# The first tile's rows chosen from the ranks, and the tile tables worked out beside that tile

## What is computed

```python
for d in range(depth):                      # depth 4, so 16 leaves
    logits = xf @ Wr[off:off + cnt].T + br[off:off + cnt]
    sel = take_along_axis(logits, leaf)
    leaf = leaf * 2 + (sel > 0)
h = gelu(xf @ W1[leaf] + b1[leaf])          # 512 -> 2048
y = h @ W2[leaf] + b2[leaf]                 # 2048 -> 512
out = x + y                                 # each row by its own leaf's expert
```

## Time and profile before

| | us |
|---|---|
| median of 3 runs | 629.48 |
| lowest and highest | 628.8 and 632.06 |
| profiled execution, its time | 632.86 |
| its span, first to last instruction | 630.9 |
| PE busy in the span | 549.9 |
| DVE busy | 191.2 |
| ACT busy | 162.4 |
| POOL busy | 62.1 |

### The profile page before, as it was taken

One profiled execution on the slowest core, in us unless ns is written; L12 is line 12 of the kernel. 1 busy time (PEld: TensorE's weight loads), 2 busy tenths in 40 slices (PEclk: granted clock), 3 DMA queues, 4 the chain that ended last, 5 costly groups with the idle time before them and its releaser, 6 DMA issues.

```text
span 630.9 us, 9966 instructions
## 1 busy us (share of the span) xinstructions
PE 549.9 (87%) x3098; PEld 288.6 (46%) x3098; DVE 191.2 (30%) x597; ACT 162.4 (26%) x548; POOL 62.1 (10%) x88
## 2 busy tenths in 40 slices
PE   2877787889899999998599999978898788987994
PEld 1544555543447466444355555524444244443352
DVE  5997776661520100266611111100111001110100
ACT  1667777111201011003022222211222012210311
POOL 3000000030000000000021121111101111011021
PEclk9979999999999999999799999988999799897998
DMA  5169900000201010023069999999999999999940
GB/s 116 13 229 431 404 3 16 18 0 1 84 3 65 0 66 0 10 60 104 1 245 422 420 425 419 426 424 426 428 426 418 422 429 425 420 422 424 428 157 5
DMA packets 24917, 145.66 MB, mean 231 GB/s; under 512 B 10303, under 2 KB 12553, under 8 KB 16706
## 3 DMA queue, kind: packets, MB, share of 16 engines
q1 hardware_dynamic: 21698, 142.91, 55.1%
q0 software_dynamic: 3200, 2.50, 2.0%
HBM read 142.38 MB, written 4.72 MB: 233 GB/s over the span
## 4 chain that ended last, share of the span: by engine, by line
PE 53%; DMA 24%; DVE 8%; ACT 6%; issue 5%; ACTq 2%; POOL 0%; SPq 0%; DVEq 0%; POOLq 0%
DMA w<-in_L_ffn_W 24%; PE P L913 15%; PE P L809 8%; PE P L961 7%; PE P L819 7%; PE P L828 3%; ACT H L513 2%; ACT H L507 2%; PE P L663 2%; PE P L930 2%; DVE stats L1085 2%; PE P L772 1%; PE P L771 1%; PE P L768 1%; PE P L785 1%
## 5 line engine op out<-in xcount | busy, mean ns | idle before, releaser
L913 PE MATMUL P<-w,H 128*64 128x512 f32 x512 | 132.2, 663 | 25.3 <-DMA w<-in_L_ffn_W 24.8
L961 PE MATMUL P<-w,FB 128*64 128x256 f32 x1024 | 114.3, 381 | 0.0
L599 ACT ACTIVATE FB<-P,G 128x64 f32<-128x64 f32 x256 | 55.8, 329 | 179.1 <-PE P L930 179.1
L1338 DVE COPY H<-P 128x512 f32<-128x512 f32 x32 | 22.1, 692 | 259.5 <-PE P L913 259.5
L961 PEld LDWEIGHTS P<-w,FB 128*64 128x64 f32 x1024 | 72.0, 137 | 37.4 <-issue 2.9
L913 PEld LDWEIGHTS P<-w,H 128*64 128x64 f32 x512 | 39.1, 151 | 98.6 <-issue 78.7
L663 PE MATMUL P<-H 125*125 125x500 bf16 x176 | 60.0, 418 | 18.5 <-ACT H L513 17.9
L1067 DVE TENSOR_SCALAR H<-iota,small 125x626 bf16<-125x626 f16 x176 | 60.1, 381 | 14.2 <-issue 8.9
L809 PE MATMUL P<-G,XT 128*125 128x512 f32 x120 | 52.0, 592 | 0.0
L663 PEld LDWEIGHTS P<-H 125*125 125x125 bf16 x176 | 25.4, 144 | 44.5 <-ACT H L513 30.6
L819 PE MATMUL P<-C,H 125*128 125x313 f32 (+1 forms) x160 | 42.4, 425 | 0.0
(11 more groups left out here) (283 smaller groups left out, 435.5 us busy)
## 6 DMA issues: line engine op xcount, KB each, us to landing
w<-in_L_ffn_W SPq DMA_DIRECT2D x64, 2048.0 KB, 29.1
G<-in_L_gnn_W SPq DMA_DIRECT2D x3, 1024.0 KB, 5.3
xs<-in_x SPq DMA_DIRECT2D x1, 1120.0 KB
out<-xs SPq DMA_DIRECT2D x5, 224.0 KB
normed_rows<-xn SPq DMA_DIRECT2D x5, 224.0 KB
out<-XT,C POOLq DMA_INDIRECT x17, 10.7
H<-in_L_gnn_W_conv SPq DMA_DIRECT2D x1, 256.0 KB, 9.1
XT<-in_L_gnn_W_lin SPq DMA_DIRECT2D x1, 256.0 KB, 2.8
```

Source lines behind the costliest of these rows:

```text
L599: g = nc.scalar.activation(hT[:, m, :], P[:, 3 + rd, c * SA:(c + 1) * SA], ACT.Gelu, bias=bT[b][:, m:m + 1])
L913: mm = nc.tensor.matmul(P[g * SA:(g + 1) * SA, h, :], xT[b][:, k, :], w1a[:, k, h, g], start=(k == 0), stop=(k == KD - 1))
L961: mm = nc.tensor.matmul(P[g * SA:(g + 1) * SA, 7, 0:256], hT[:, m, :], w2_sb[b][:, m, g * 256:(g + 1) * 256], start=False, stop=(m == MH - 1))
L1338: nc.vector.tensor_copy(h_sb[:, t, :].rearrange("p (r n) -> p r n", r=4), P[:, t, :].rearrange("p (n r) -> p r n", r=4)).then_inc(s_hc, 1)
```

## The change

1. DVE copies the ranks to SBUF (`rank`) beside the counts, adds EMPTY to those of nodes that are not expert 0's (`not0`, `rank0`), and makes `sel` from that at once. Tile 0 is always expert 0 with 64 rows, so no table is needed. The rest of the chain follows behind `sel`.
2. `keep_warm(4)` is gone. The selected rows go to bank 0 instead of bank 6.
3. DVE copies the selected rows behind L1258, and the turned rows (`copy_inputs(0, 0)`) behind the number of pairs, ahead of the table, the offsets and the turned biases.
4. `number_rows` (the former L1308 to L1328) stands within tile 0's copies on DVE, behind its second hidden half and ahead of tile 1's turned rows. Its products (`slot_tokens`, into bank 5) stand on PE between the second and the third quarter of tile 0's second layer. The turn of tile 1's rows, with its wait for the gather, follows tile 0's last quarter.
5. On PE and DVE the first pair of tiles is written out ahead of the loop, which starts at 1; PE's wait for the table and its load of the number of pairs stand between them.

POOL's, ACT's and SP's programs are unchanged.

```diff
@@ tensor
-            keep_warm(4, xn[0:NC, 0, :], bank=4)
             pe.wait_ge(s_sel, 1)
-                    mm = nc.tensor.matmul(P[g * SA:(g + 1) * SA, 6, 0:256], sel[0:NC, c, :], xn[0:NC, c, g * 256:(g + 1) * 256],
+                    mm = nc.tensor.matmul(P[g * SA:(g + 1) * SA, 0, 0:256], sel[0:NC, c, :], xn[0:NC, c, g * 256:(g + 1) * 256],
                                           start=(c == 0), stop=(c == NCH - 1))
             mm.then_inc(s_xrow, 1)
             pe.wait_ge(s_xrowc, 1)
             turn_rows(0)
-            pe.wait_ge(s_slots, 1)
-            for which, n, at in ((0, SA, slots), (1, SB_, slotsB), (2, SB_, slotsB)):
...
-            mm.then_inc(s_rows, 1)
-            pe.wait_ge(s_table, 1)
-            last = pe.value_load(npairs_t[0:1, 0:1], min_val=NE // 2 - 1, max_val=MAX_PAIRS - 1)
             pe.wait_ge(s_b2z, 1)
             pe.wait_ge(s_b2, 16)
+            def slot_tokens():
+                pe.wait_ge(s_slots, 1)
...
+                mm.then_inc(s_rows, 1)
             def tile(p, b, end=False):
                 i = 2 * p + b
                 more = end and b == 0
+                first = isinstance(p, int) and i == 0
...
-                if not (end and b):
+                if not (first or end and b):
                     pe.wait_ge(s_xr, 16 * i + 16)
                     turn_rows(i + 1)
...
                 for q in range(1, 4):
+                    if first and q == 2:
+                        slot_tokens()
                     second_a(q)
+                if first:
+                    pe.wait_ge(s_xr, 16)
+                    turn_rows(1)
...
-            with pe.Fori(0, last) as p:
+            for b in range(2):
+                tile(0, b)
+            pe.wait_ge(s_table, 1)
+            last = pe.value_load(npairs_t[0:1, 0:1], min_val=NE // 2 - 1, max_val=MAX_PAIRS - 1)
+            with pe.Fori(1, last) as p:
@@ vector
+            rank, not0, rank0 = sv(0, NCH, NE), sv(90, NCH), sv(100, NCH)
+            link(ts(not0[0:NC, :], leaf[0:NC, :, 0], -EMPTY, EMPTY, ALU.mult, ALU.add))
             dve.wait_ge(s_rank, 1)
-            rank = P[0:NC, 6, 0:NCH * NE].rearrange("p (c e) -> p c e", e=NE)
+            nc.vector.tensor_copy(rank[0:NC], P[0:NC, 6, 0:NCH * NE].rearrange("p (c e) -> p c e", e=NE))
             link(nc.vector.tensor_copy(cnt16[:, :], P[:, 6, NCH * NE:(NCH + 1) * NE]))
+            link(tt(rank0[0:NC, :], rank[0:NC, :, 0], not0[0:NC, :], ALU.add))
+            tt(sel[0:NC], iota[0:NC, 0:SA].unsqueeze(1).to_broadcast([NC, NCH, SA]),
+               rank0[0:NC, :].unsqueeze(2).to_broadcast([NC, NCH, SA]), ALU.is_equal).then_inc(s_sel, 1)
...
             link(nc.vector.tensor_reduce(le[0:NC, :], val[0:NC], AX.X, ALU.add))
-            tt(sel[0:NC], iota[0:NC, 0:SA].unsqueeze(1).to_broadcast([NC, NCH, SA]),
-               le[0:NC, :].unsqueeze(2).to_broadcast([NC, NCH, SA]), ALU.is_equal).then_inc(s_sel, 1)
+            dve.wait_ge(s_xrow, 1)
+            nc.vector.tensor_copy(x_row, P[:, 0, 0:256]).then_inc(s_xrowc, 1)
...
             link(ts(last2, more[:, 5:6], 2.0, float(NE - 2), ALU.mult, ALU.add))
+            copy_inputs(0, 0)
             link(tt(top[:, :], big[:, :], iota[:, 0:NE], ALU.mult))
...
-            dve.wait_ge(s_table, 1)
-            dve.wait_ge(s_xrow, 1)
-            nc.vector.tensor_copy(x_row, P[:, 6, 0:256]).then_inc(s_xrowc, 1)
-            copy_inputs(0, 0)
-            link(ts(in_tile[0:NC], offs[0:NC], 0.0, None, ALU.is_ge))
...
+            def number_rows():
+                link(ts(in_tile[0:NC], offs[0:NC], 0.0, None, ALU.is_ge))
...
             def tile_copies(p, b, end=False):
...
+                if isinstance(p, int) and i == 0:
+                    number_rows()
                 if not (end and b):
                     copy_inputs(i + 1, 1 - b)
-            with dve.Fori(0, last) as p:
+            for b in range(2):
+                tile_copies(0, b)
+            with dve.Fori(1, last) as p:
```

More of the change, by code:

```diff
@@ L889, in _ @@
             turn_rows(0)
-            pe.wait_ge(s_slots, 1)
-            for which, n, at in ((0, SA, slots), (1, SB_, slotsB), (2, SB_, slotsB)):
[L892 to L895, removed]
-            mm.then_inc(s_rows, 1)
-            pe.wait_ge(s_table, 1)
-            last = pe.value_load(npairs_t[0:1, 0:1], min_val=NE // 2 - 1, max_val=MAX_PAIRS - 1)
             pe.wait_ge(s_b2z, 1)
             pe.wait_ge(s_b2, 16)
+            def slot_tokens():
+                pe.wait_ge(s_slots, 1)
+                for which, n, at in ((0, SA, slots), (1, SB_, slotsB), (2, SB_, slotsB)):
+                    for c in range(NCH):
+                        for g in range(2 if which == 2 else 128 // n):
+                            mm = nc.tensor.matmul(P[g * n:(g + 1) * n, 5, 256 + which * 32:256 + which * 32 + TAB + 2], at[0:NC, c, :],
+                                                  tok_tile[0:NC, :, c], start=(c == 0), stop=(c == NCH - 1), skip_group_check=True)
+                mm.then_inc(s_rows, 1)
             def tile(p, b, end=False):
@@ L1252, in _, with copy_inputs @@
             link(tt(jump[0:NC, :], jump[0:NC, :], home[0:NC, :], ALU.subtract))
-            link(tt(val[0:NC], rank, cap[0:NC, :].unsqueeze(1).to_broadcast([NC, NCH, NE]), ALU.is_ge))
+            link(tt(val[0:NC], rank[0:NC], cap[0:NC, :].unsqueeze(1).to_broadcast([NC, NCH, NE]), ALU.is_ge))
             link(tt(val[0:NC], val[0:NC], jump[0:NC, :].unsqueeze(1).to_broadcast([NC, NCH, NE]), ALU.mult))
             link(tt(val[0:NC], val[0:NC], home[0:NC, :].unsqueeze(1).to_broadcast([NC, NCH, NE]), ALU.add))
-            link(tt(val[0:NC], val[0:NC], rank, ALU.add))
+            link(tt(val[0:NC], val[0:NC], rank[0:NC], ALU.add))
             link(tt(val[0:NC], val[0:NC], leaf[0:NC], ALU.mult))
             link(nc.vector.tensor_reduce(le[0:NC, :], val[0:NC], AX.X, ALU.add))
-            tt(sel[0:NC], iota[0:NC, 0:SA].unsqueeze(1).to_broadcast([NC, NCH, SA]),
-               le[0:NC, :].unsqueeze(2).to_broadcast([NC, NCH, SA]), ALU.is_equal).then_inc(s_sel, 1)
+            dve.wait_ge(s_xrow, 1)
+            nc.vector.tensor_copy(x_row, P[:, 0, 0:256]).then_inc(s_xrowc, 1)
+            def copy_inputs(i, b):
+                dve.wait_ge(s_xT, i + 1)
+                nc.vector.tensor_copy(xT[b].rearrange("p (g j) s -> p j g s", g=2),
+                                      P[:, 6, 256:512].rearrange("p (j g s) -> p j g s", j=2, g=2)).then_inc(s_xTc, 1)
             link(ts(more[:, 0:5], iota[:, 0:5], 2.0, cnt16[:, NE - 1:NE], ALU.mult, ALU.is_lt))
@@ L1329, in _ @@
             dve.wait_ge(s_b1Tc, 1)
             last = dve.value_load(npairs_t[0:1, 0:1], min_val=NE // 2 - 1, max_val=MAX_PAIRS - 1)
+            def number_rows():
+                link(ts(in_tile[0:NC], offs[0:NC], 0.0, None, ALU.is_ge))
+                size = cmpq
+                link(ts(size, pos, float(NE), float(SB_), ALU.is_lt, ALU.mult))
+                link(ts(size, size, float(SA), None, ALU.add))
+                link(tt(tok_tile[0:NC], offs[0:NC], size[0:NC, :].unsqueeze(2).to_broadcast([NC, TAB + 2, NCH]), ALU.is_lt))
+                link(tt(in_tile[0:NC], in_tile[0:NC], tok_tile[0:NC], ALU.mult))
+                link(tt(offs[0:NC], offs[0:NC], in_tile[0:NC], ALU.mult))
+                link(nc.vector.tensor_reduce(spos[0:NC, :], offs[0:NC].rearrange("p t c -> p c t"), AX.X, ALU.add))
+                tt(tok_tile[0:NC], in_tile[0:NC], token[0:NC, :].unsqueeze(1).to_broadcast([NC, TAB + 2, NCH]), ALU.mult)
+                tt(slots[0:NC], iota[0:NC, 0:SA].unsqueeze(1).to_broadcast([NC, NCH, SA]),
+                   spos[0:NC, :].unsqueeze(2).to_broadcast([NC, NCH, SA]), ALU.is_equal)
+                tt(slotsB[0:NC], iota[0:NC, SA:ROWS].unsqueeze(1).to_broadcast([NC, NCH, SB_]),
+                   spos[0:NC, :].unsqueeze(2).to_broadcast([NC, NCH, SB_]), ALU.is_equal).then_inc(s_slots, 1)
+                link(ts(half_ofB, part, float(SB_), -2.0, ALU.is_ge, ALU.add))
+                dve.wait_ge(s_rows, 1)
+                for which, per, of in ((0, 2.0, half_of), (1, 4.0, quarter_of), (2, 2.0, half_ofB)):
+                    rows = 2 * SB_ if which == 2 else 128
+                    v = P[0:rows, 5, 256 + which * 32:256 + which * 32 + TAB + 2]
+                    link(ts(rows_f[0:rows, which, :], v, 0.5, EMPTY, ALU.is_lt, ALU.mult))
+                    link(stt(rows_f[0:rows, which, :], v, per, rows_f[0:rows, which, :], ALU.mult, ALU.add))
+                    ts(rows_i[0:rows, which, :], rows_f[0:rows, which, :], of[0:rows, :], None, ALU.add).then_inc(s_idx, 1)
```

## The result

| | before | after |
|---|---|---|
| median, us | 631.88 (14 runs) | 629.67 (14 runs) |
| lowest to highest | 628.80 to 633.03 | 627.98 to 631.38 |
| profiled execution: time, span | 632.86, 630.9 | 629.54, 627.6 |

The ratio of the times is 0.997, with a 95% interval of 0.9956 to 0.9985: a gain of 1.9 us (0.9 to 2.8). The forecast was a gain of 3.8 us and a time of 625.7; its interval of times holds 629.67, but the gain is half of what was forecast. (The medians differ by 2.2, the ratio gives 1.9.) Of the 4.0 us by which the time was missed, 2.4 lie in the starting point: more runs of the kernel before moved its median from 629.48 to 631.88. The other 1.6 are the subject here.

What follows compares the result with a forecast made beforehand. The prediction took the saturated DMA weight stream to set the end: the later of T1 + 19.7 and T2 moves from 340.6 to 336.8, and that 3.8 us off 629.48 gives 625.7; range 620.8 to 630.0.

Steps and rivals of the forecast that it cites:

- position: Weight stream after its first batch of reloads: the later of T1 + 19.7 and T2; 340.6 before, 336.8 after.
- T1: SP's issue of the reload for tile 2's weights: forecast at 309.65, against 320.89 before.
- Part 1: Selection from the ranks, ahead of tile 0: PE starts tile 0 at 301.5, against 312.29, 10.8 us earlier.
- Part 2: Tables beside tile 0: 1.9 us of new wait for the first hidden half; SP's first reload 11.2 us earlier.
- Part 3: Row numbers inside tile 0's second layer: no wait for slots, products 1.7 us, gather of tile 1's rows issued at 321.0.
- Part 4: Gather of tile 1's rows under the weight stream: takes 6.0 us from its issue, landing at 327.0.
- L: Time of the gather of tile 1's rows from its issue: 6.0 us, between 2.4 and 9.06.
- Part 5: Tile 1 starts cold at 328.2: half clock costs 2.35 us, and T2 is 336.8.
- The sum: Stream after its first batch: max(309.65 + 19.7, 336.8) = 336.8, against 340.6 before; gain 3.8 us.
- T2: SP's issue of the reload for tile 3's weights: forecast at 336.8, against 337.00 before.
- the dry spell of the stream: Weight stream without work between its first and second batch of reloads: a gap of about 7.4 us.
- C: Rival: the gather of tile 1's rows takes near 9.06 us; T2 = 339.9, gain 0.7, 628.8; chance 0.17.

Runs made afterwards that it cites:

- e2_warm9: The changed kernel with 9 unread products on PE ahead of the wait for tile 1's rows; ratio 0.9921 to the kernel before.
- e1_warm: The changed kernel with 6 unread products on PE ahead of the wait for tile 1's rows; ratio 0.9972 to the kernel before.
- e1_hold_first: The changed kernel, but SP's first reload also waits for tile 0's first quarter of the second layer; ratio 0.9970 to the kernel before.
- e1_hold_w2: The changed kernel, but SP holds back the reload of W2 until tile 1's rows are in; ratio 0.9894 to the kernel before.

## Why the prediction was half right

What bounds the kernel: right. The position separates the five kernels at 0.5 to 2.4 from the three at 5.9 to 11.4, and in the first group only e2_warm9 stands out; that T1 could be moved by 5 us without effect is what the rule says.

Part 1: tile 0 at 302.1, forecast 301.5. The chain of small steps came out within 0.2 us. "A clock that falls in the short pauses" was given 0 to 1.3 us and taken as 0; it fell ahead of tile 0 in this profile. What that costs can be read from the eight profiles with this selection: tile 0's first stretch took 7.05, 7.22, 6.15 and 6.21 us in four and 4.51 in the other four, with the same PE program up to there. In those other four the clock had fallen as well, but was back in time (e1_warm: granted 0.76 in 295 to 302, 1.00 in 302 to 306). The same code may find either clock.

Part 2: L1352 at 308.33, forecast 307.05, T1 at 310.94 for 309.65. The forecast let DVE's tables end last; in the profile PE did (L1352 waited 1.82 us for L913), because of the half clock. In e1_warm, with tile 0 warm, DVE's tables and register loads ended last, as forecast, with T1 at 310.24 (the two loads took 1.36 us, its upper bound, for the 0.9 taken). Harmless in itself, but the gather's issue stands in the same chain.

Part 3: right. No wait for the slots, products 1.92 us long (forecast 1.7, bounds 1.24 and 2.48), gather 11.55 us after T1 (forecast 11.35), so at 322.49 instead of 321.0.

Part 4 is the step that failed: L, the gather's time from issue to use, taken as 6.0 (2.4 without load, 3.6 for the load) between bounds of 2.4 and 9.06, measured 7.6, 7.8 in e1_warm and 7.5 in e1_hold_first, and 3.0 without load. So 0.6 us were missed without load, where the forecast had read the second, smaller gather, and 1.0 us in the load, 4.6 for 3.6. The argument by halves (a gather has one packet a row, a scatter two, so it pays half of the scatter's 7.2 us) started from a misreading of the earlier trace rows. In the kernel before, the two gathers are alone on DMA from 317 to 320:

```profile
DMA packets 80, 0.13 MB, mean 43 GB/s; under 512 B 47, under 2 KB 47, under 8 KB 80
```

None of their packets is between 512 B and 2 KB; 33 are above, of 4 KB on average. So the 1270 packets of that size in the earlier trace rows are not the gathers', and a gather has no packet for each row. That 3.6 came near 4.6 was luck. The rule of the Trainium skill ("DMA: Bandwidth & Descriptors", section "Queues, rings and completion order") is that an engine alternates between its queues packet by packet. The prediction worked out 4.4 us for the load by it, nearer to 4.6, but with eight packets of the gather on each engine. 33 large packets on 16 engines are about two each, for which the same working gives 1.1 us as an estimate; so the traces do not bear out that price. They show where the time goes in part: the gather's first packet starts 4.5 us after its issue in the changed kernel and 2.0 in e1_hold_w2, so 2.5 of the 4.6 us pass before it has moved anything. What holds it up there is open.

Part 5: the cold start cost 1.62 us (7.86 against 6.24), forecast 2.35. This error of 0.7 went the other way.

The sum: T2 was 2.4 us later than forecast (339.2 for 336.8): 1.5 from the gather's late issue, 1.6 from L, less 0.7 from tile 1. Of the 1.5, 0.7 is the clock ahead of tile 0 that was put at nothing (with tile 0 at full clock, e1_warm issues the gather at 321.78 for 322.49), and 0.5 the register loads. So the gain by the rule fell from 3.8 to 1.4. The mechanism, the dry spell of the stream, was right (forecast 7.4 us, by the same sum 8.6), and what happened lies between the forecast's lower end (1.8) and the rival in which all is given back (C, 0.7). The forecast itself was a difference of two times near 340 whose terms were each known to one or two microseconds. The range said so; the point and the 0.64 for a clear gain did not.

## What to carry to other kernels

Where a saturated DMA stream sets the end, price a change by when the stream starts and by the first time that it can run dry (here by the later of T1 + 19.7 and T2), and look for the second as hard as for the first: a start brought forward by 10 us was worth 2 here. A small transfer that moves from before a stream to beside it has to be priced at its loaded latency (7.6 us for 3.0); if an engine waits for it, fetch it another way, or hold the stream back for it, which here was worth 4.8 us.

## What was not expected of the hardware

A pause of 2.08 us right after 5.4 us of unread products was followed by half clock for part of tile 1's first stretch (6.21 against 4.51 us); in e1_hold_w2 a pause of 2.61 us was not followed by it. Why the one was and the other wasn't is open. And of eight profiles with the same PE program up to tile 0, four have tile 0's first stretch at least partly at half clock and four at full clock: a single profile doesn't tell whether a place is cold.
